# Second layer's down products written token-major, with gelu's output as the weights

## The chip, the cores and the metric

The kernel runs on one core of a Trainium2 chip. The metric is the device time of one execution in microseconds (us). A core has TensorE (in the profile PE for its products and PEld for its weight loads), VectorE (DVE), ScalarE (ACT), GpSimd (POOL) and SyncE (SP), which starts most transfers. The engines run their own instruction streams and meet only at semaphores.

## The reference

Four layers work on x, 4 samples of 256 tokens with 64 features. The change lies in the second half of the third one, a mixture of experts in which each sample picks two of eight experts for all its tokens:

```python
rw_tok = jnp.broadcast_to(routing_weights[:, None, :], (B, S, E)).reshape(N, E)
top_w, top_i = jax.lax.top_k(rw_tok, K)                  # K = 2
top_w = jax.nn.softmax(top_w, axis=-1)
h = jax.nn.gelu(jnp.einsum('nd,edf->enf', xf, W1) + b1[:, None, :], approximate=False)
y = jnp.einsum('enf,efd->end', h, W2) + b2[:, None, :]   # F = 128, D = 64
w_dense = jnp.zeros((N, E), x.dtype).at[jnp.arange(N)[:, None], top_i].add(top_w)
out = jnp.einsum('ne,end->nd', w_dense, y).reshape(B, S, D)
out = _layer_norm(out + x, gamma, beta)
```

Then `t = t + out`, and the fourth layer (attention with gates, then a second mixture of experts with one expert for each token) follows.

## The kernel before

Everything stays in the core's memory. A tensor is held either token-major (128 tokens down the partitions, 64 features along a row; a sample has TB = 2 such tiles) or feature-major (64 features down the partitions, 256 tokens along a row). Each engine's program is written out by hand, and every meeting of two engines is a counted semaphore. TensorE's program also holds products that nobody reads, with `onesb` as both operands (`keep_warm`), at fixed places and in fixed numbers.

The stage of the change, sample by sample (b = 0 to 3):

- Selection: ScalarE and VectorE copy the two chosen experts' matrices into `W1sel` (64 features and a bias row, by 128) and `W2sel` (128 by 64, already scaled with the expert's share `tw`). VectorE then works out `b2sel`, the mixed output bias, one column of 64 features for each sample.
- Up (L748): for each of the two experts one product, `W1sel` as the weights, the sample's tokens `XFb` (256 of them) moving. Result 128 by 256, twice, in one bank.
- Gelu (L1121, ScalarE): bank to `H2`, which lies in `bias_mem`.
- Down (L761): `W2sel` as the weights, `H2` moving, both experts added in the bank: 64 features by 256 tokens.
- Bias step (L1491, VectorE): bank plus `b2sel` to `UT`, which lies in `half_mem`.
- Turn (L770): two transposes through TensorE bring `UT` token-major into another bank.
- Sum (L1497, VectorE): turned bank plus `XNb` gives `U`, in `mid_mem`. After U of samples 0 to 2 VectorE takes the statistics of samples 0 and 1 (L1344, L1352, L1355), then U of sample 3, then the statistics of samples 2 and 3. GpSimd turns variances into factors (L405), and the two halves are normalised on VectorE (L1372) and ScalarE (L1051), scaled (L1509), added (L1511) and normalised again for the next layer.

An fp32 product is two instructions on TensorE, each with its own weight load; an fp32 transpose is one. GpSimd's addition at L437 (`X3b`) waits for the first bias step. Behind its last turn TensorE runs 34 `keep_warm` products (L453) and then `features_c` (L780), the turns for the next layer, as soon as their input is normalised. Names of the profile: `stack_mem` in this stage is `W1sel` and `W2sel`, `Cs` is the table of constants with the unit matrix `ident`.

Of the kernel before, what the change touches and what calls it, by code (L numbers as in the profile page):

```python
# [14 lines left out]
P = 128  # L15
B, HW, C = 4, 16, 64
N = HW * HW
TB = N // P
# [18 lines left out]
E2, F2, TOPK = 8, 128, 2  # L37
# [3 lines left out]
SLOTS = E3 * CAP3  # L41
# [5 lines left out]
IOTA_AT = NH * TB * SPAN // 2  # L47
# [4 lines left out]
ALU = mybir.AluOpType  # L52
# [24 lines left out]
def hybrid_kernel(nc, x, xt, w8, w0, wa, wg, w3, w2a, w2b, cst, bias_q, bias_k, lnw, out):  # L77
    ctx = ExitStack()
    with ctx:
# [5 lines left out]
        def sem(name):  # L85
            if name not in sems:
                sems[name] = ctx.enter_context(nc.semaphore(name))
            return sems[name]

        bank = [ctx.enter_context(nc.psum_tensor(f"bank{i}", [P, 512], F32)) for i in range(8)]  # L90
# [15 lines left out]
        half_mem = sb("half_mem", [P, 4992])  # L106
# [32 lines left out]
        ident = Cs[:, CST["ident"]]  # L139
# [79 lines left out]
        W2sel = view(stack_mem, P, B * TOPK, C)  # L219
        chosen = sb("chosen", [P, B * TOPK])  # L220
        b2w = sb("b2w", [C, B * TOPK, E2])
        b2sel = sb("b2sel", [C, B])
        H2 = view(bias_mem, P, B, TOPK * N)
        X4 = view(half_mem, P, T, C)
        UT = half_mem[0:C, IOTA_AT + SLOTS:IOTA_AT + SLOTS + B * N]
        U = view(mid_mem, P, T, C)
        gb = sb("gb", [P, 2, C])
        X3b = view(mid_mem, P, T, C)
# [125 lines left out]
        def _(pool):  # L354
# [77 lines left out]
                rstd("b", half)  # L432


            pool.wait_ge(sem("ut"), 1)
            pool.wait_ge(sem("gb_landed"), 16)
            pool.tensor_tensor(X3b[:, :, :], X3[:, :, :], gb[:, 1, :].unsqueeze(1).to_broadcast([P, T, C]), ALU.add) \  # L437
                .then_inc(sem("x3b"), 1)
# [9 lines left out]
        def _(pe):  # L448
# [138 lines left out]
            for t in range(T):  # L587
                last = pe.matmul(bank[7][:, t * C:t * C + C], XN1[:, t * P:t * P + P], W0s[:, W0["wv1"]],
                                 start=True, stop=True)
# [78 lines left out]
            for n in range(B * NH + LAG):  # L668
                b, h = divmod(n, NH)
# [31 lines left out]
            for i in range(B + 2):  # L701
# [9 lines left out]
                if 0 <= i - 1 < B:  # L711
                    b = i - 1
# [10 lines left out]
            for b in range(B):  # L723
# [14 lines left out]
                      start=True, stop=True).then_inc(sem("pe_routing"), 1)  # L738
            keep_warm(WARM["selection"], bank[7])

            for i in range(B + 2):
                if i < B:
                    b = i
                    pe.wait_ge(sem("sel_a"), 2 * b + 1)
                    pe.wait_ge(sem("sel_v"), 2 * b + 1)
                    pe.wait_ge(sem("b_xf"), B)
                    for k in range(TOPK):
                        last = pe.matmul(bank[b][:, k * N:k * N + N], W1sel[:, TOPK * b + k, :],  # L748
                                         XF["b"][:, b * N:b * N + N], start=True, stop=True)
                    last.then_inc(sem("up2"), 1)  # L750
                if 0 <= i - 1 < B:
                    b = i - 1
                    pe.wait_ge(sem("gelu"), b + 1)
                    pe.wait_ge(sem("sel_a"), 2 * b + 2)
                    pe.wait_ge(sem("sel_v"), 2 * b + 2)
                    if b == 0:
                        pe.wait_ge(sem("r_spread_read"), 2)
                    if b >= 2:
                        pe.wait_ge(sem("ut"), b - 1)
                    for k in range(TOPK):  # L760
                        last = pe.matmul(bank[4 + b % 2][0:C, 0:N], W2sel[:, TOPK * b + k, :],  # L761
                                         H2[:, b, k * N:k * N + N], start=(k == 0), stop=(k == TOPK - 1))
                    last.then_inc(sem("down2"), 1)
                if 0 <= i - 2 < B:
                    b = i - 2
                    pe.wait_ge(sem("ut"), b + 1)
                    if b >= 2:
                        pe.wait_ge(sem("u"), b - 1)
                    for q in range(TB):
                        last = pe.transpose(bank[6 + b % 2][:, q * C:q * C + C], UT[:, b * N + q * P:b * N + q * P + P],  # L770
                                            ident[0:C, 0:C])
                    last.then_inc(sem("u_turned"), 1)


            def features_c(b):
# [68 lines left out]
            for i in range(B + 2):  # L844
# [8 lines left out]
                if i >= 2:  # L853
                    pe.wait_ge(sem("d_xf"), i - 1)
                    for t in range(TB * (i - 2), TB * (i - 1)):
                        last = pe.matmul(bank[4][:, t * E3:t * E3 + E3], XF["d"][:, t * P:t * P + P],  # L856
                                         WAs[:, WA["gate"]], start=True, stop=True)
# [92 lines left out]
            for h in range(2):  # L950
                for q in range(T // 2):
                    t = h * T // 2 + q
                    if q % 2 == 0:
                        pe.wait_ge(sem("zt_v" if h else "zt"), q // 2 + 1)
                    last = pe.matmul(bank[h][:, q * C:q * C + C], ZT[:, t * P:t * P + P], twice[:, :],
                                     start=True, stop=True)
# [250 lines left out]
        def _(dve):  # L1207
# [264 lines left out]
            for i in range(1, B * TOPK, TOPK):  # L1472
# [10 lines left out]
                                   ALU.mult))  # L1483
            dve.tensor_reduce(b2sel[:, :], b2w[:, :, :].rearrange("p (b k) e -> p b (k e)", b=B), AX.X, ALU.add) \
                .then_inc(sem("b2sel"), 1)
            for i in range(B + 1):
                if i < B:
                    b = i
                    dve.wait_ge(sem("down2"), b + 1)
                    dve.wait_ge(sem("b2sel"), 1)  # L1490
                    dve.tensor_scalar(UT[:, b * N:b * N + N], bank[4 + b % 2][0:C, 0:N], b2sel[:, b:b + 1],  # L1491
                                      None, ALU.add) \
                        .then_inc(sem("ut"), 1)
                if i >= 1:
                    b = i - 1
                    dve.wait_ge(sem("u_turned"), b + 1)
                    dve.tensor_tensor(U[:, TB * b:TB * b + TB, :],  # L1497
                                      bank[6 + b % 2][:, 0:TB * C].rearrange("p (q c) -> p q c", q=TB),
                                      XN["b"][:, TB * b:TB * b + TB, 0:C], ALU.add).then_inc(sem("u"), 1)
                if i == B - 1:  # L1500
                    stats("u", U, "u", B // 2, 0)
# [268 lines left out]
```

## Time and profile before

| | us |
|---|---|
| median of 3 executions | 170.19 |
| lowest and highest | 169.01, 171.38 |
| the profiled execution | 168.97 |
| its span, first to last instruction | 167.1 |

| engine | busy, us | share of the span |
|---|---|---|
| PE | 146.9 | 88% |
| PEld | 102.9 | 62% |
| DVE | 111.3 | 67% |
| ACT | 75.1 | 45% |
| POOL | 50.8 | 30% |

A share of busy time is a mean over many short stages, and `keep_warm` counts as busy. All times below are from the start of the span; the stage of the change lies at 91 to 103 us.

### The profile page before, as it was taken

What the parts mean: (1) busy time and instruction counts of PE and PEld (TensorE: products, weight loads), DVE (VectorE), ACT (ScalarE), POOL (GpSimd) and SP (SyncE); (2) the same over time, 40 slices, a digit from 0 to 9 for tenths busy, and PEclk for the clock granted to TensorE, in tenths of its full rate; (3) what the DMA queues carried; (4) which work ended last, traced back from release to release, by engine and by line L of the source; (5) the groups of instructions that cost most, each with busy time, mean ns of one, the idle gap of its engine ahead of it and who ended that gap; (6) DMA issues with size and microseconds to landing.
All of it is one profiled execution on the core that took longest, in us unless ns stands there. A gap on an engine that the chain in (4) does not pass through costs nothing. (4 is left out here: it accounts for less than half of the span.)

```text
span 167.1 us, 3148 instructions
## 1 busy us (share of the span) xinstructions
PE 146.9 (88%) x1087; PEld 102.9 (62%) x1087; DVE 111.3 (67%) x385; ACT 75.1 (45%) x197; POOL 50.8 (30%) x78
## 2 busy tenths in 40 slices
PE   7999977799999998799787999967999899899920
PEld 2598736598888886588234554445665637678620
DVE  2027664987879898536644538947969289696873
ACT  3445605335353545451636550397535433555140
POOL 7051359786555657110400023520002200000000
PEclk9999999999999999999999999999999959999985
DMA  5993044373450000058000000000000000000002
GB/s 147 358 417 99 4 127 93 96 201 110 129 132 2 6 0 4 0 117 329 15 0 0 0 0 0 2 0 0 6 0 0 4 0 0 0 0 4 0 0 65
DMA packets 7098, 10.30 MB, mean 62 GB/s; under 512 B 2719, under 2 KB 5608, under 8 KB 6698
## 3 DMA queue, kind: packets, MB, share of 16 engines
q1 hardware_dynamic: 6880, 9.72, 19.2%
q10 hardware_dynamic: 202, 0.38, 0.9%
q8 instruction: 9, 0.15, 0.4%
q14 instruction: 7, 0.06, 0.1%
HBM read 8.52 MB, written 1.57 MB: 60 GB/s over the span
## 5 line engine op out<-in xcount | busy, mean ns | idle before, releaser
L453 PE MATMUL bank<-onesb 128*128 128x512 bf16 x142 | 36.7, 406 | 1.1 <-DVE onesb L1221 1.1
L453 PEld LDWEIGHTS bank<-onesb 128*128 128x128 bf16 x142 | 14.0, 105 | 16.1 <-issue 3.5
L418 POOL TENSOR_TENSOR half_mem<-identb,nm 128x256 bf16<-128x256 bf16 x32 | 19.5, 614 | 11.5 <-DVE nm L1302 11.3
L1302 DVE TENSOR_REDUCE nm<-bank 128x2 bf16<-128x352 f32 x32 | 16.3, 516 | 4.0 <-PE bank L607 3.7
L1037 ACT ACTIVATE mid_mem<-mid_mem 128x352 f32<-128x352 f32 x20 | 9.8, 496 | 18.4 <-DVE mid_mem L1313 18.4
L625 PE MATMUL bank<-stack_mem 72*128 72x176 bf16 x64 | 13.7, 240 | 0.1
L631 PE MATMUL bank<-half_mem,onesb 128*128 128x176 bf16 x64 | 13.5, 239 | 0.0
L605 PE MATMUL bank<-stack_mem 72*128 72x176 bf16 x64 | 12.7, 241 | 0.9 <-DVE nm L1302 0.9
L607 PE MATMUL bank<-half_mem,identb 128*128 128x176 bf16 x64 | 12.6, 239 | 0.0
L1313 DVE TENSOR_TENSOR mid_mem<-bank,bias_mem 128x352 f32<-128x352 f32 x20 | 10.3, 542 | 0.0
L629 PE MATMUL bank<-bias_mem,identb 128*128 128x176 bf16 x72 | 9.3, 238 | 0.0
L605 PEld LDWEIGHTS bank<-stack_mem 72*128 72x128 bf16 x64 | 6.2, 98 | 3.2 <-DVE nm L1302 2.1
L405 POOL TENSOR_TENSOR ln_rsd<-ln_ved,mhalf 128x4 f32<-128x4 f32 x2 | 2.1, 1027 | 18.1 <-DVE ln_ved L1355 18.1
L648 PE MATMUL bank<-mid_mem 128*32 128x176 f32 x128 | 6.4, 319 | 0.6 <-ACT mid_mem L1033 0.6
L625 PEld LDWEIGHTS bank<-stack_mem 72*128 72x128 bf16 x64 | 6.2, 97 | 0.6 <-issue 0.4
L1600 DVE TENSOR_SCALAR one_hot<-half_mem,sid 128x1280 fp32r<-128x1280 f32 x8 | 6.5, 882 | 0.0
L607 PEld LDWEIGHTS bank<-half_mem,identb 128*128 128x128 bf16 x64 | 6.3, 98 | 0.1
L1033 ACT ACTIVATE mid_mem<-bank 128x352 f32<-128x352 f32 x12 | 5.4, 454 | 1.7 <-PE bank L631 1.7
L631 PEld LDWEIGHTS bank<-half_mem,onesb 128*128 128x128 bf16 x64 | 6.2, 97 | 0.0
L1228 DVE TENSOR_REDUCE nmax<-bank 128x2 f32<-128x512 f32 x4 | 2.8, 688 | 5.1 <-PE bank L469 5.1
L923 PE MATMUL bank<-stack_mem,mid_mem 128*128 128x160 f32 x32 | 5.4, 312 | 0.8 <-ACT stack_mem L1162 0.7
L629 PEld LDWEIGHTS bank<-bias_mem,identb 128*128 128x128 bf16 x72 | 6.1, 98 | 0.0
(279 smaller groups left out, 330.8 us busy)
## 6 DMA issues: line engine op xcount, KB each, us to landing
stack_mem<-qk_parts SPq DMA_DIRECT2D x21, 96.0 KB
bias_mem<-bias_q SPq DMA_DIRECT2D x1, 1408.0 KB, 8.2
bias_mem<-bias_k SPq DMA_DIRECT2D x1, 1408.0 KB, 11.7
mid_mem<-w SPq DMA_DIRECT2D x1, 1024.0 KB, 7.5
qk_parts<-half_mem SPq DMA_DIRECT2D x4, 192.0 KB, 2.7
qk_parts<-half_mem SPq DMA_DIRECT2D x4, 128.0 KB, 2.4
mid_mem<-w2b SPq DMA_DIRECT2D x1, 512.0 KB, 8.4
Cs<-cst SPq DMA_DIRECT2D x1, 336.0 KB, 4.3
```

Source lines behind the costliest of these rows:

```text
L418: pool.tensor_tensor(diag1[:, b % 2, h, :].rearrange("p (q k) -> p q k", q=TB), identb[:, :].unsqueeze(1).to_broadcast([P, TB, P]), nm1[:, ...
L453: pe.matmul(idle[:, :].rearrange("p (k q) -> p k q", k=4), onesb[:, :], onesb[:, :].unsqueeze(1).to_broadcast([P, 4, P]), start=True, stop ...
L605: pe.matmul(dst, QS[:, b, h, q * P:q * P + P], KSt[:, b, h, OFF[q]:OFF[q] + SPAN], start=True, stop=False)
L607: last = pe.matmul(dst, identb[:, :], biasQb[:, h, q * SPAN:q * SPAN + SPAN], start=False, stop=True)
L625: pe.matmul(dst, KSt[:, b, h, k * P:k * P + P], QS[:, b, h, OFF[k]:OFF[k] + SPAN], start=True, stop=False)
L629: pe.matmul(dst, identb[:, :], bias_part[:, i, PE_HEADS.index(h), span], start=False, stop=False)
L631: last = pe.matmul(dst, onesb[:, :], diag1[:, b % 2, h, OFF[k]:OFF[k] + SPAN], start=False, stop=True)
L648: last = pe.matmul(bank[4 + b % 2][32 * g:32 * g + VW, c0 + OFF[k]:c0 + OFF[k] + SPAN], V1[:, TB * b + k, h, :], P1[:, (b * NH + h) % (2 * ...
L1037: act.activation(P1[:, n % (2 * QUAD), :], U1[:, n % 3, :], ACT.Exp).then_inc(sem("p1"), 1)
L1302: dve.tensor_reduce(nm1[:, n // NH, n % NH, :], bank[n % 2][:, 0:TB * SPAN].rearrange("p (q k) -> p q k", q=TB), AX.X, ALU.max, negate=Tru ...
L1313: dve.tensor_tensor(U1[:, n % 3, :], bank[2 + n % 2][:, 0:TB * SPAN], biasK[:, n % NH, :], ALU.add) \
L1600: dve.tensor_scalar(G3[:, t % 3, :], iota_f[:, :], sid[:, t:t + 1], None, ALU.is_equal) \
```

## The change

The operands of the down product change places: a block of 128 tokens of `H2` is the weights, and `W2sel` with its 64 columns moves. The result is token-major at once, so the turn and VectorE's step into `UT` go. The bias enters as one more product into the same bank: `b2sel`'s column, repeated 128 times by a stride of zero, as the weights, and the 64 by 64 unit matrix moving, once for both token blocks (128 columns) and ahead of the down products; for sample 0 it comes behind them, once for each block of tokens, with a wait for `b2sel` behind the first block. The sum at L1497 now waits for the down product itself, and GpSimd's L437 for the first U in place of the first bias step.

```diff
-            pool.wait_ge(sem("ut"), 1)
+            pool.wait_ge(sem("u"), 1)
...
-            for i in range(B + 2):
+            for i in range(B + 1):
...
                     if b >= 2:
-                        pe.wait_ge(sem("ut"), b - 1)
-                    for k in range(TOPK):
-                        last = pe.matmul(bank[4 + b % 2][0:C, 0:N], W2sel[:, TOPK * b + k, :],
-                                         H2[:, b, k * N:k * N + N], start=(k == 0), stop=(k == TOPK - 1))
+                        pe.wait_ge(sem("u"), b - 1)
+                    dst = bank[6 + b % 2][:, 0:TB * C].rearrange("p (q c) -> p q c", q=TB)
+                    bias, unit = b2sel[:, b:b + 1].to_broadcast([C, P]), ident[0:C, 0:C]
+                    if b > 0:
+                        pe.matmul(dst, bias, unit.unsqueeze(1).to_broadcast([C, TB, C]), start=True, stop=False,
+                                  skip_group_check=True)
+                    for q in range(TB):
+                        for k in range(TOPK):
+                            last = pe.matmul(dst[:, q, :], H2[:, b, k * N + q * P:k * N + q * P + P],
+                                             W2sel[:, TOPK * b + k, :], start=(b == 0 and k == 0),
+                                             stop=(b > 0 and k == TOPK - 1), skip_group_check=True)
+                        if b == 0:
+                            if q == 0:
+                                pe.wait_ge(sem("b2sel"), 1)
+                            last = pe.matmul(dst[:, q, :], bias, unit, start=False, stop=True, skip_group_check=True)
                     last.then_inc(sem("down2"), 1)
-                if 0 <= i - 2 < B:
-                    b = i - 2
-                    pe.wait_ge(sem("ut"), b + 1)
-                    if b >= 2:
-                        pe.wait_ge(sem("u"), b - 1)
-                    for q in range(TB):
-                        last = pe.transpose(bank[6 + b % 2][:, q * C:q * C + C], UT[:, b * N + q * P:b * N + q * P + P],
-                                            ident[0:C, 0:C])
-                    last.then_inc(sem("u_turned"), 1)
...
-            for i in range(B + 1):
-                if i < B:
-                    b = i
-                    dve.wait_ge(sem("down2"), b + 1)
-                    dve.wait_ge(sem("b2sel"), 1)
-                    dve.tensor_scalar(UT[:, b * N:b * N + N], bank[4 + b % 2][0:C, 0:N], b2sel[:, b:b + 1],
-                                      None, ALU.add) \
-                        .then_inc(sem("ut"), 1)
+            for i in range(1, B + 1):
                 if i >= 1:
                     b = i - 1
-                    dve.wait_ge(sem("u_turned"), b + 1)
+                    dve.wait_ge(sem("down2"), b + 1)
```

TensorE's program from the last two up products to the 34 products that nobody reads, before (a row is one product in the program; `[waits ...]` are the semaphores ahead of it):

```order
412 L748 MATMUL bank<-XFb,stack_mem 128x256 [waits b_xf,sel_v,sel_a]
413 L748 MATMUL bank<-XFb,stack_mem 128x256
414 L761 MATMUL bank<-bias_mem,stack_mem 64x256 [waits sel_v,ut,sel_a,gelu]
415 L761 MATMUL bank<-bias_mem,stack_mem 64x256
416 L770 MATMUL bank<-Cs,half_mem 128x64 [waits ut]
417 L770 MATMUL bank<-Cs,half_mem 128x64
418 L761 MATMUL bank<-bias_mem,stack_mem 64x256 [waits sel_v,ut,sel_a,gelu]
419 L761 MATMUL bank<-bias_mem,stack_mem 64x256
420 L770 MATMUL bank<-Cs,half_mem 128x64 [waits u,ut]
421 L770 MATMUL bank<-Cs,half_mem 128x64
422 L770 MATMUL bank<-Cs,half_mem 128x64 [waits u,ut]
423 L770 MATMUL bank<-Cs,half_mem 128x64
```

And TensorE's program now, from sample 0's down product to the same place (L747 is the up product, L766 the down product, L762 and L772 the bias):

```order
404 L766 MATMUL bank<-stack_mem,bias_mem 128x64 [waits sel_v,r_spread_read,sel_a,gelu]
405 L766 MATMUL bank<-stack_mem,bias_mem 128x64
406 L772 MATMUL bank<-Cs,b2sel 128x64 [waits b2sel]
407 L766 MATMUL bank<-stack_mem,bias_mem 128x64 x2
408 L772 MATMUL bank<-Cs,b2sel 128x64
409 L747 MATMUL bank<-XFb,stack_mem 128x256 [waits b_xf,sel_v,sel_a]
...
414 L747 MATMUL bank<-XFb,stack_mem 128x256
415 L762 MATMUL bank<-Cs,b2sel 128x128 [waits sel_v,u,sel_a,gelu]
416 L766 MATMUL bank<-stack_mem,bias_mem 128x64 x4
417 L762 MATMUL bank<-Cs,b2sel 128x128 [waits sel_v,u,sel_a,gelu]
418 L766 MATMUL bank<-stack_mem,bias_mem 128x64 x4
```

The turns are gone, the down product has become five products in place of two, and sample 0's holds a wait for `b2sel` in its middle.

VectorE's program from `b2sel` to the end of the first statistics, before:

```order
178 L1484 TENSOR_REDUCE b2sel<-b2w 64x4
179 L1491 TENSOR_SCALAR half_mem<-bank,b2sel 64x256 x2
180 L1497 TENSOR_TENSOR mid_mem<-bank,XNb 128x128
181 L1491 TENSOR_SCALAR half_mem<-bank,b2sel 64x256
182 L1497 TENSOR_TENSOR mid_mem<-bank,XNb 128x128
183 L1491 TENSOR_SCALAR half_mem<-bank,b2sel 64x256
184 L1497 TENSOR_TENSOR mid_mem<-bank,XNb 128x128
185 L1344 BN_STATS ln_stu<-mid_mem 128x6 x4
```

And now (L1491 is here the sum U, and L1345 the statistics):

```order
178 L1485 TENSOR_REDUCE b2sel<-b2w 64x4
179 L1491 TENSOR_TENSOR mid_mem<-bank,XNb 128x128 x3
180 L1345 BN_STATS ln_stu<-mid_mem 128x6 x4
181 L1353 BN_AGGR ln_mvu<-ln_stu 128x2 x4
182 L1356 TENSOR_SCALAR ln_veu<-ln_mvu 128x4
183 L1491 TENSOR_TENSOR mid_mem<-bank,XNb 128x128
```

The four bias steps are gone; the sums and the statistics keep their order, and sample 3's bias step no longer stands ahead of sample 2's sum.

## Rows read from the trace of the kernel before

**Rows 1.** The page's head and TensorE's granted clock in 40 slices (tenths).

```profile
span 167.1 us, 3148 instructions
...
PEclk9999999999999999999999999999999959999985
```

**Rows 2.** The chain that ended last, in order of time: start us, length us, what.

```profile
93.99 1.08 PE bank L761 x4
95.07 1.06 PE bank L748 x4
96.13 1.01 PE bank L761 x4
97.14 0.27 PE bank L770 x2
...
99.74 1.02 PE bank L761 x4
...
100.78 0.48 DVE half_mem L1491
101.26 0.20 DVE mid_mem L1497
...
138.68 3.20 PE bank L877 x15
```

**Rows 3.** Timeline, 93 to 103 us: start us, us, engine, line, out<-in, [idle before].

```profile
94.49 0.21 DVE L1484 TENSOR_REDUCE b2sel<-b2w 64x4 f32<-64x64 f32 x1
...
95.66 1.26 POOL L437 TENSOR_TENSOR mid_mem<-X,gb 128x512 f32<-128x512 f32 x1 [13.57 <-DVE half_mem L1491]
...
98.50 0.60 ACT L1121 ACTIVATE bias_mem<-bank 128x512 f32<-128x512 f32 x1 [1.74 <-PE bank L748]
...
101.18 0.27 DVE L1497 TENSOR_TENSOR mid_mem<-bank,XNb 128x128 f32<-128x128 f32 x1
...
101.58 6.65 PE L453 MATMUL bank<-onesb 128*128 128x512 bf16 x30
...
102.42 0.17 DVE L1355 TENSOR_SCALAR ln_veu<-ln_mvu 128x4 f32<-128x4 f32 x1
102.49 0.28 DVE L1497 TENSOR_TENSOR mid_mem<-bank,XNb 128x128 f32<-128x128 f32 x1
```

**Rows 4.** Timeline, 105 to 110 us.

```profile
105.53 0.42 DVE L1511 TENSOR_TENSOR half_mem<-stack_mem,mid_mem 128x256 f32<-128x256 f32 x1
...
105.69 3.40 PE L453 MATMUL bank<-onesb 128*128 128x512 bf16 x15
...
108.78 1.65 ACT L1051 ACTIVATE stack_mem<-half_mem,ln_nbc,ln_rsc 128x128 f32<-128x128 f32 x4 [1.76 <-POOL ln_nbc L409]
...
109.80 0.41 PE L780 MATMUL bank<-Cs,stack_mem 128*128 128x128 f32 x2 [0.71 <-ACT stack_mem L1051]
```

**Rows 5.** Timeline at 74 and at 159 us: products with 128 weight columns and few moving ones.

```profile
74.27 1.08 PEld L697 LDWEIGHTS bank<-XNa,S_PT 128*128 128x128 f32 x8
74.48 1.00 PE L697 MATMUL bank<-XNa,S_PT 128*128 128x65 f32 x8
...
75.52 0.17 DVE L1414 RECIPROCAL rdena<-bank 128x2 f32<-128x2 f32 x1 [2.00 <-PE bank L697]
...
159.09 0.97 PEld L955 LDWEIGHTS bank<-twice,XHL 128*128 128x128 f32 x8 [0.97 <-issue]
```

**Rows 6.** Groups by line and form: count, busy us, mean ns, idle before.

```profile
L697 PEld LDWEIGHTS bank<-XNa,S_PT 128*128 128x128 f32 x32 | 4.1, 192 | 0.2
...
L761 PEld LDWEIGHTS bank<-bias_mem,stack_mem 128*64 128x64 f32 x16 | 1.9, 136 | 2.2 <-ACT bias_mem L1121 0.8 <-issue 0.7
```

**Rows 7.** Windows: us, busy us and instructions of each engine, clock, DMA share, GB/s.

```profile
94.00:98.00 4.00, 4.00 (x17) 2.41 (x18) 1.78 (x6) 1.01 (x2) 1.26 (x1) 1.00 0.00 0
...
134.00:136.00 2.00, 2.00 (x15) 0.79 (x13) 1.83 (x9) 0.26 (x1) 0.00 (x0) 0.55 0.00 0
136.00:138.00 2.00, 2.00 (x7) 0.78 (x6) 1.90 (x7) 1.11 (x4) 0.00 (x0) 0.60 0.00 0
```

**Rows 8.** Timeline, 136 to 144 us: VectorE's comparisons for the gather at L877.

```profile
136.88 6.49 DVE L1600 TENSOR_SCALAR one_hot<-half_mem,sid 128x1280 fp32r<-128x1280 f32 x8
```

More of the change, by code:

```diff
@@ L224, in hybrid_kernel @@
         X4 = view(half_mem, P, T, C)
-        UT = half_mem[0:C, IOTA_AT + SLOTS:IOTA_AT + SLOTS + B * N]
         U = view(mid_mem, P, T, C)
```

## The prediction

> **What bounds the kernel now.** Four views, in this order. The page's head gives the span, 167.1 us, and shows that TensorE's clock was at its upper level nearly everywhere [rows 1]. The chain of work that ended last says who holds the stage of the change: from 93.99 us it runs through TensorE alone, without a gap, over down, up, down, turn, up, down, turn, down (1.08, then 1.06 for each of two up products, 1.01 for each further down product, 0.27 for each of two turns), until 100.76 us; then over VectorE's bias step of sample 3 (0.48) into the sum U of sample 2, which began at 101.18 us [rows 2, 3]. From there VectorE holds the chain with the statistics. The timeline shows what stands close beside it, and the windows give the clock. So this stage is bound by TensorE up to U of sample 2, and then by VectorE. Each tenth of a microsecond by which U of sample 2 starts earlier is one for the whole kernel, if nothing named below is late in its place.
>
> The profiled execution took 168.97 us, 1.87 more than its span and 1.22 less than the median of 170.19. I work out a difference on the profiled execution and take it off the median.
>
> **The change part by part.**
>
> *Removed from the path.* Two turns, 2 x 0.27 = 0.54 us; VectorE's bias step of sample 3 ahead of sample 2's sum, 0.48 us less what overlaps (the sum began 0.40 us after that step did) [rows 2, 3]. The other three bias steps ran beside TensorE's products and give nothing.
>
> *Changed on the path.* A down product was four instructions (two products, two for fp32 each) with 256 moving columns in 1.01 us. It becomes eight with 64 moving columns, and two for the bias with 128 columns. The trace has the same form elsewhere. L697 has 128 weight columns and 65 moving ones: eight weight loads took 1.08 us, of which the last is 0.192 long [rows 5, 6]; so from one to the next (1.08 - 0.192) / 7 = 0.127 us. L955 has 64 moving columns: (0.97 - 0.192) / 7 = 0.111 us [rows 5, 6]. I take 0.12, between the two, and call it p. The bias product's instructions have the same number of weight columns and 128 moving; a column of an fp32 instruction costs 1.01 / (4 x 256), about 1 ns [rows 2], so the stream would want 0.13 and I count them as p too. A stride of zero in the weights has no row in this trace; its bounds are p and, if such loads could not run ahead at all, the 0.192 of a whole load. Four instructions on the path up to U of sample 2 (of samples 1 and 2) could so cost up to 4 x 0.07 = 0.3 us more, and four of sample 0 as much again. I take p, since all other loads with 128 columns in fp32 run under the products before them.
>
> The size of a load is where a page has something to say against this change. Loads of 64 columns lasted 136 ns here and loads of 128 columns 192 ns [rows 6]. The Trainium skill, in "TensorE: Matmul & The Clock Gate", section "LDWEIGHTS (loading the stationary operand)", says that a load's time goes with the number of weight columns and not with the contraction, about columns / 1.2 ns; by that rule exchanging the operands makes each load dearer by 53 ns, and the trace agrees with 56. The same rule, taken as the spacing of a stream bound by loads, would be 0.107 us.
>
> *Added to the path.* In sample 0's down product TensorE waits for `b2sel` behind its first four instructions. These start at 93.99 us, with gelu, and are through their loads at 94.35 + 0.12. `b2sel` starts at 94.49 and takes 0.21 [rows 3]: 94.70, and 0.04 for the signal. So eight instructions stand behind 94.74 us. Behind this wait in TensorE's queue are the second token block and the up products of samples 2 and 3, and ScalarE's gelu of samples 2 and 3 waits for those.
>
> *The sum.* By this the next up product starts at 94.74 + 8p, and U of sample 2 at 94.74 + 8p (rest of sample 0) + 1.06 (up) + 10p (sample 1) + 1.06 (up) + 9p (up to the last load of sample 2) + 0.36. The last term is the time from the last load to VectorE's start at L697: the last load began at 74.27 + 7 x 0.127 = 75.16, VectorE at 75.52 [rows 5]. Together 97.22 + 27p. With p = 0.12 that is 100.46 us where it was 101.18: a gain of 0.7 us. With 0.127 it is 0.5, with 0.111 it is 1.0.
>
> *What is late next.* Three covers are thin.
> - U of sample 3 can start at 97.22 + 37p = 101.66 us. VectorE reaches it behind the first statistics, formerly at 102.49 [rows 3], now 0.7 earlier, at 101.8: covered by 0.1.
> - The 34 products that nobody reads start behind sample 3's down product, at 96.86 + 38p = 101.4 us, formerly at 101.58. They last as before, to 105.69 + 3.40 = 109.09 less 0.2, so 108.9. The next layer's turn, formerly at 109.80 behind ScalarE [rows 4], is due at 109.1: covered by 0.2. TensorE stood idle 0.71 us there, so no gain much above 0.9 could come through this place.
> - Gelu of sample 3 ran at 98.50, beside TensorE [rows 3]; it moves behind the later up product, to about 99.1 to 99.7. Sample 3's down product is due at 100.3. Covered by 0.6; uncovered it would cost one for one.
>
> *Free of charge.* GpSimd's addition at L437 waits for U of sample 0 in place of the first bias step: from 95.66 to about 96.3, over at 97.6; L1511, which reads it, runs at 105.53 [rows 3, 4], and GpSimd's next work, the first factors, comes at 102 us. Its cover is some 4 us. No transfer and no queue of SyncE is touched.
>
> **The rivals.**
>
> *Exposed loads, the one that ends slower.* Every new down instruction carries its own load of 128 columns and streams 64, so the load is longer than the stream (0.192 against about 0.065). If a load did not run under the product before it, p would be 0.192: U of sample 2 at 97.22 + 27 x 0.192 = 102.4, U of sample 3 at 104.3 against 102.49, and the products that nobody reads would start 2.6 late against 0.71 of idle time. The largest delay, 1.9 us, would come through: 172.1 us. It decides from p = 0.142 to 0.147, where these terms equal the times of before. Against it: 0.111 and 0.127 in rows 5. For it: weights that are gelu's fresh output, repeated columns in every step, and the exchange of two weight regions (64 rows for the bias, 128 for the rest). Chance 0.07.
>
> *A shorter spacing.* The Trainium skill, in the section "Back-to-back issue gap" of the page named above, gives about 81 ns for a load and product pair in a stream with 128 columns, against 0.111 and 0.127 us in rows 5, which are fp32. What such a spacing would do here: with p = 0.08, U of sample 2 comes at 99.4, a gain of 1.8, of which sample 3's later product and the next turn let most pass, since those 34 products would begin 1.7 earlier as well. That is 168.4 us. The rows speak against it, with L697 and L955 both above 0.11. Chance 0.05.
>
> *The clock falls elsewhere.* In the profiled execution the clock was low once, over parts of 134 to 136 and 136 to 138 us, a granted 0.55 and 0.60 [rows 7], so at 1.2 GHz for some 3.4 us in all; ahead of it TensorE had short turns and products with 8 columns. There it cost next to nothing, since TensorE waited for VectorE anyway. VectorE's comparisons then pace the gather at 6.49 / 8 = 0.81 us each [rows 8], while TensorE needs 2.5 x 3.20 / 15 = 0.53 at full clock [rows 2], and 1.07 at half. Were the low stretch to fall on the gather, its 3.4 us would lose 3.4 / 0.81 x (1.07 - 0.81) = 1.1 us. The executions of before spread over 2.4 us, and the profiled one was the fastest; a shift by 0.7 us can put more or fewer of them there. With the gain in it: 169.5 + 1.1 = 170.6 us. Chance 0.17. In 94 to 98 us the clock was full [rows 7]; as the products of 65 columns at 74 us kept it, I expect no fall within the stage.
>
> *Nothing comes through.* The wait for `b2sel`, the slower bias loads and the two thin covers each take a few tenths and leave 0.0 to 0.2: 170.1 us. Chance 0.13.
>
> **How the numbers follow.** The forecast, a gain of 0.7 on 170.19, is 169.5 us, chance 0.58; its own range is 168.7 to 170.2, from a gain of 0.5 to 1.0 and half a microsecond for a median of three runs that lie 2.4 apart. The range that should hold 8 times in 10 adds the clock and the lost gain: 168.3 to 171.2. Two per cent, 3.4 us, is about what a measurement of this kernel can tell from no change; neither of the named cases reaches 166.8 or 173.6. For what I have not seen I leave 0.03 on the fast side and 0.03 on the slow one, and 0.94 within.
>
> **What the profile of the changed kernel would show.** The loads of the down product at 0.11 to 0.13 us from one to the next, and the bias instructions no slower. Sample 0's down product interrupted at about 94.5 and on from 94.74, the next up product 0.6 us later than before. U of sample 2 at about 100.5, U of sample 3 straight behind the first statistics, with VectorE idle before it for under 0.1. The first factors on GpSimd 0.7 earlier. At the next layer's turn an idle time of about 0.2 where there was 0.71, ended by ScalarE. From there the same rows as before, shifted by 0.7. The prediction is wrong if loads of the broadcast column are slow, if TensorE is still busy with the products that nobody reads when ScalarE has the next layer's input, or if the clock's low stretches fall on other work in most executions of one kernel and not of the other.

## The result, and the profile after

The changed kernel took 176.83 us in the median of 4 executions (175.07 to 181.83), the kernel before 170.22 (169.01 to 171.38). The ratio is 1.0355, 95% interval 1.0234 to 1.0475: slower by 3.5%, where 169.5 us and a small gain were forecast. Ratios here leave out executions more than 1.5% above the fastest of their kernel, and with them some of those in which the clock fell, so where the spread itself is the finding, I give all times.

The head of the page after, to be held against [rows 1]:

```profile
span 175.3 us, 3174 instructions
...
PEclk9999999999999999999999555699999999999995
```

The clock was low in the middle, where it had been full. The chain that ended last, through the stage (start us, length us, what), against [rows 2]:

```profile
95.34 0.48 PE bank L772 x2
95.83 1.04 PE bank L766 x4
96.87 0.62 PE bank L772 x2
97.49 2.00 PE bank L747 x4
99.49 0.72 PE bank L762 x2
100.22 1.90 PE bank L766 x8
102.11 1.81 PE bank L747 x4
103.93 0.72 PE bank L762 x2
104.65 1.90 PE bank L766 x8
106.55 0.72 PE bank L762 x2
107.27 1.90 PE bank L766 x8
109.17 9.12 PE bank L452 x34
118.29 0.23 PE bank L781 x2
```

TensorE holds the chain as before, but an up product (L747), which the change does not touch, takes 2.00 and 1.81 us where it took 1.06. The windows name the reason (busy us and instructions of PE, PEld, DVE, ACT, POOL; then the granted clock, DMA share, GB/s), against [rows 7]:

```profile
92.00:95.50 3.50, 2.99 (x16) 2.20 (x14) 1.93 (x10) 2.60 (x8) 0.00 (x0) 1.00 0.00 0
95.60:99.00 3.40, 3.40 (x12) 2.64 (x11) 0.29 (x1) 0.00 (x0) 1.10 (x1) 0.50 0.00 0
99.00:102.40 3.40, 3.40 (x13) 2.71 (x12) 0.25 (x1) 0.60 (x1) 0.16 (x1) 0.50 0.00 0
102.40:105.80 3.40, 3.40 (x12) 2.40 (x10) 0.04 (x1) 1.82 (x2) 0.00 (x0) 0.50 0.00 0
105.80:109.20 3.40, 3.40 (x15) 2.97 (x15) 1.35 (x10) 0.26 (x2) 1.02 (x1) 0.50 0.02 5
109.20:112.60 3.40, 3.40 (x9) 1.21 (x8) 3.23 (x17) 0.30 (x1) 1.36 (x2) 0.50 0.00 0
112.70:116.00 3.30, 3.30 (x17) 1.50 (x16) 3.09 (x21) 1.54 (x6) 1.38 (x2) 1.00 0.00 0
```

From 95.6 us, one microsecond into the stage, TensorE ran at 1.2 GHz, through the whole stage and into the products that nobody reads, and was back at 2.4 GHz only there. From the fall on it counts as busy without a gap. Where the 8.2 us of span went: the stage began at 94.58 us in place of 93.99 (0.6, from work ahead of it that the change leaves alone); from its first down product to the products that nobody reads 14.4 us in place of 7.6 (6.8); from there to the next layer's turn, now at 118.13, 9.2 in place of 8.2 (0.9); from there to the end 57.2 in place of 57.3.

The timeline shows the stage's start, where the clock fell, against [rows 3]:

```profile
94.58 0.52 PEld L766 LDWEIGHTS bank<-stack_mem,bias_mem 128*128 128x128 f32 x4 [0.80 <-ACT bias_mem L1122]
...
95.34 0.30 PEld L772 LDWEIGHTS bank<-Cs,b2sel 64*128 64x128 f32 x2 [0.24 <-DVE b2sel L1485]
```

Ahead of the fall TensorE idled for gelu, ran four thin instructions (loads of 0.52 us in all, so (0.52 - 0.19) / 3 = 0.11 us apart, as forecast) and stopped again for `b2sel`. So only one microsecond of changed instructions lay ahead of the fall; the up products and the wait for gelu ahead of them stand in the kernel before too, where the clock stayed up.

### The profile page after: what moved, and what is told of

Read it like the earlier page. It is cut to its first block and busy times, and to the rows that moved or that the text cites. A ratio compares the mean times of both kernels' runs of the same rounds, so it can differ in the third digit from the quotient of the medians.

```text
span 175.3 us, 3174 instructions
## 1 busy us (share of the span) xinstructions
PE 155.5 (89%) x1105; PEld 110.7 (63%) x1105; DVE 109.7 (63%) x381; ACT 75.1 (43%) x197; POOL 50.8 (29%) x78
## 5 line engine op out<-in xcount | busy, mean ns | idle before, releaser
L452 PE MATMUL bank<-onesb 128*128 128x512 bf16 x142 | 37.6, 414 | 1.0 <-DVE onesb L1222 1.0
L452 PEld LDWEIGHTS bank<-onesb 128*128 128x128 bf16 x142 | 14.4, 107 | 16.6 <-issue 4.3
L1491 DVE TENSOR_TENSOR mid_mem<-bank,XNb 128x128 f32<-128x128 f32 x4 | 1.2, 292 | 11.9 <-PE bank L766 9.7
L766 PE MATMUL bank<-stack_mem,bias_mem 128*128 128x64 f32 x32 | 7.7, 411 | 0.4 <-ACT bias_mem L1122 0.4
L766 PEld LDWEIGHTS bank<-stack_mem,bias_mem 128*128 128x128 f32 x32 | 6.8, 309 | 1.6 <-ACT bias_mem L1122 0.8
L878 PE MATMUL bank<-one_hot,XHL 128*128 128x512 f32 (+1 forms) x24 | 6.1, 382 | 0.3 <-DVE one_hot L1594 0.3
```

The source lines that it names most:

```text
L452: pe.matmul(idle[:, :].rearrange("p (k q) -> p k q", k=4), onesb[:, :], onesb[:, :].unsqueeze(1).to_broadcast([P, 4, P]), start=True, stop ...
L766: last = pe.matmul(dst[:, q, :], H2[:, b, k * N + q * P:k * N + q * P + P], W2sel[:, TOPK * b + k, :], start=(b == 0 and k == 0), stop=(b ...
L878: last = pe.matmul(bank[c][:, 0:width], XHL[:, t, :, :].rearrange("p k c -> p (k c)"), G3[:, t % 3, at:at + width], start=(t == 0), stop=( ...
```

## The experiments

Four suspects: the thin streams of the down product (A), the stop for `b2sel` (B), the repeated bias column as weights (C), and, after the first four runs, the change of rows at the bias product (D). Below, "the stage" is the time from the first down product to the first of the 34 products that nobody reads, in the profiled execution: 7.6 us before, 14.4 after. "Low" is a granted clock of 0.5, 1.2 GHz.

**The changed kernel again.** No edit.

> The changed kernel as it is, once more, beside the others. All theories: 175 to 178 us in most executions, mean granted clock 0.93 to 0.95, as in its first four.

Measured: 174.91, 174.99, 176.22, 176.41 and 181.29 us; ratio to the kernel before 1.0299 (1.0238 to 1.0359). With the first four, nine executions and none below 174.9. In the profiled one, of 181.29 us, the clock had been low once before, long ahead of the change (10.6 to 31.1 us), which made the stage 7 us late. It fell again at 106.2 us, inside the stage (first down product at 101.77), and the stage took 11.6 us:

```profile
PEclk9965555999999999999999985599999999999995
```

**Streams of double width.** The second copy falls into columns that nobody reads.

```diff
-dst = bank[6 + b % 2][:, 0:TB * C].rearrange("p (q c) -> p q c", q=TB)
+both = bank[6 + b % 2][:, 0:TB * 2 * C].rearrange("p (q w c) -> p q w c", q=TB, w=2)
+dst = both[:, :, 0, :]
...
-last = pe.matmul(dst[:, q, :], H2[...], W2sel[:, TOPK * b + k, :], ...)
+last = pe.matmul(both[:, q, :, :], H2[...], W2sel[:, TOPK * b + k, :].unsqueeze(1).to_broadcast([P, 2, C]), ...)
```

> The changed kernel with each down product streaming 128 columns in place of 64: the expert's 64 columns twice, the second copy into a part of the bank that nobody reads. Loads, waits and order are unchanged, the result too. Thin streams (theory A: the clock falls because the stage's products stream few columns behind long loads): the clock stays at its upper level through the stage, the stage takes what was forecast (U of sample 2 about 6.5 us behind the first down product), 169 to 171 us. The wait (theory B: TensorE's stop for b2sel in sample 0's down product makes it fall) or the repeated bias column (theory C): the low stretch stays, 175 to 178 us.

Measured: 169.71, 171.43, 171.48 and 174.96 us; ratio 1.0051 (0.9957 to 1.0146). Doubling the columns that TensorE streams, with nothing else changed, takes away most of the loss in three executions of four. In the profiled one, of 174.96, the clock still fell in the stage, at 98.0 us (first down product at 95.16). So A has a part, but is not all of it.

**Sample 0's bias behind its down products.** No stop in the middle.

```diff
-                        if b == 0:
-                            if q == 0:
-                                pe.wait_ge(sem("b2sel"), 1)
-                            last = pe.matmul(dst[:, q, :], bias, unit, start=False, stop=True, ...)
+                    if b == 0:
+                        pe.wait_ge(sem("b2sel"), 1)
+                        last = pe.matmul(dst, bias, unit.unsqueeze(1).to_broadcast([C, TB, C]), start=False, stop=True, ...)
```

> The changed kernel with sample 0's bias as one product behind its four down products, so that b2sel is there before TensorE comes to it; two bias instructions fewer and next to no stop in the middle. Theory A (thin streams): still slow, some tenths of a microsecond less than the changed kernel, 174.5 to 177.5. Theory B (the wait): full clock in the stage and 169 to 170.5 us. Theory C (the repeated column): as A.

Measured: 174.29, 174.47, 176.05 and 181.97 us; ratio 1.029 (1.0196 to 1.0385). As A and C had it: without the stop the clock still fell in the stage, in the profiled execution at 106.1 us, 3.1 us behind the first down product. It was low from 10.6 to 31.0 us as well, as in the repeat of the changed kernel.

**The stop alone, in the kernel before.**

```diff
                     for k in range(TOPK):
+                        if b == 0 and k == 1:
+                            pe.wait_ge(sem("b2sel"), 1)
                         last = pe.matmul(bank[4 + b % 2][0:C, 0:N], W2sel[...], H2[...], ...)
```

> The kernel before with one wait more: TensorE waits for b2sel between the two products of sample 0's down product. All else is as before. Theory A (thin streams) and C (repeated column): the clock as in the kernel before, the wait costs at most some 0.2 to 0.4 us, 169.5 to 171.5. Theory B (the wait alone lets the clock fall): a low stretch in the stage, 173 to 177 us.

Measured: 169.15 to 171.40 us, ratio 1.0003 (0.992 to 1.0085). The stop costs the stage 0.3 us (7.9 for 7.6) and, among streams of 256 columns, does not bring the clock down. B alone is out.

**No bias products.** The kernel leaves out the output bias, and with it the stop for `b2sel`.

```diff
-                    if b > 0:
-                        pe.matmul(dst, bias, unit..., start=True, stop=False, ...)
...
-                        if b == 0:
-                            if q == 0:
-                                pe.wait_ge(sem("b2sel"), 1)
-                            last = pe.matmul(dst[:, q, :], bias, unit, start=False, stop=True, ...)
```

> The changed kernel without the bias products and without the wait for b2sel; the output bias of the second layer's experts is left out of the computation. Theory C (the repeated column as weights): full clock, 168 to 170 us. Theory B (the wait): the same. Theory A (thin streams of 64 columns): the clock still falls in the stage, 173 to 176.5 us, lower than the changed kernel by the ten bias instructions, 1 to 2 us at low clock.

Measured: 168.09, 168.64, 168.85 us and one of 179.53 at a mean clock of 0.991, so disturbed by something else than the clock; ratio 0.9913 (0.9838 to 0.9988). A alone is out, as far as three executions tell: the streams are as thin as in the changed kernel, and in the profiled one the clock stayed up in the stage, which took 5.4 us:

```profile
PEclk9999999699999999999999999999999969999975
```

As taking the stop away did not help by itself, the bias product matters, and its row says how. In the run with both early edits (next but one), at full clock:

```profile
97.81 0.29 PEld L763 LDWEIGHTS bank<-Cs,b2sel 64*128 64x128 f32 x2 [0.33 <-issue]
97.81 0.48 PE L763 MATMUL bank<-Cs,b2sel 64*128 64x128 f32 x2
...
98.22 0.19 PEld L767 LDWEIGHTS bank<-stack_mem,bias_mem 128*128 128x128 f32 x1
98.22 0.38 PE L767 MATMUL bank<-stack_mem,bias_mem 128*128 128x128 f32 x1
```

The first load of the bias and the first load behind it start together with their products, where the loads between them start ahead, beside the product before. Two instructions take 97.81 to 98.22 = 0.41 us, where I had 0.24. The bias is over 64 rows, the products around it over 128 and 65. That was theory D: the change of rows keeps the loads from running ahead.

**The bias over 128 rows.**

```diff
-        b2sel = sb("b2sel", [C, B])
+        b2sel = sb("b2sel", [P, B])
...
-                    bias, unit = b2sel[:, b:b + 1].to_broadcast([C, P]), ident[0:C, 0:C]
+                    bias, unit = b2sel[:, b:b + 1].to_broadcast([P, P]), ident[:, 0:C]
...
+            dve.memset(b2sel[C:P, :], 0.0).then_inc(sem("b2sel_low"), 1)
```

> The changed kernel with the bias product over all 128 rows: b2sel gets 64 rows of zeros below, and the first 64 columns of the full unit matrix move. As many instructions, columns and loads, the same wait in sample 0, the same result. Theory D (a product with 64 rows between products with 128 rows cannot have its weights loaded ahead, nor can the one behind it, which costs some 0.3 us a sample and lets TensorE stream so little that the clock falls): the two bias instructions take 0.11 us each, the clock stays up in the stage in most executions, 169 to 171 us. Theory C (the repeated column itself): loads as slow as before and the clock low, 175 to 178 us. Theory A (thin streams alone): the gaps go but the clock still falls, 174 to 176 us.

Measured: twelve executions in two groups, five at 169.52 to 170.61 us and seven at 173.75 to 177.14, with mean clocks of 0.959 to 0.977 and 0.920 to 0.947; the median is 174.24. So D's edit alone frees less than half of the executions. In the profiled one, of 174.99, the clock fell at 95.8 us, 1.1 us behind the first down product.

**Double width and sample 0's bias behind.** The bias at 64 rows.

> The changed kernel with both edits of the first two runs: each down product streams its 64 columns twice, and sample 0's bias is one product behind its down products. The bias stays at 64 rows. If the fall of the clock goes by how much of the stage TensorE streams, two edits that each raise that share keep the clock up more often than either alone: 169.5 to 171 us with the slow switches of rows still in it. If the bias product as such lets the clock fall: 172 us or more.

Measured: eight executions at 168.38 to 169.86 us, one at 176.30 and one at 181.47 (the latter at a mean clock of 0.985); ratio 0.9912 (0.9859 to 0.9966). The bias product as such does not bring the clock down. In the profiled execution the stage took 7.8 us at full clock, no less than in the kernel before.

**The bias over 128 rows, sample 0's behind.** Streams of 64 columns.

> The changed kernel with the bias product over 128 rows and sample 0's bias as one product at the end, so neither switch of rows nor stop in the middle; the streams of the down product stay at 64 columns. Theory D (switches of rows): full clock and what was forecast, 168.5 to 170 us, U of sample 2 some 6.1 us behind the first down product. Theory A (thin streams alone): the clock falls, 173 to 175 us.

Measured: eight executions at 167.60 to 170.66 us, two at 175.54 and 176.81; ratio 0.9935 (0.9876 to 0.9993). The profiled execution, 167.60 us, is the changed kernel's idea at full clock. The clock of its page, and its timeline:

```profile
PEclk9999999999999999999999999999999999999995
...
93.96 0.97 PEld L766 LDWEIGHTS bank<-stack_mem,bias_mem 128*128 128x128 f32 x8 [0.80 <-ACT bias_mem L1123]
...
96.05 0.39 PE L762 MATMUL bank<-Cs,b2sel 128*128 128x128 f32 x2
96.16 0.97 PEld L766 LDWEIGHTS bank<-stack_mem,bias_mem 128*128 128x128 f32 x8
...
96.27 1.00 PE L766 MATMUL bank<-stack_mem,bias_mem 128*128 128x64 f32 x8
...
99.29 0.29 DVE L1493 TENSOR_TENSOR mid_mem<-bank,XNb 128x128 f32<-128x128 f32 x1 [1.69 <-PE bank L766]
...
100.21 7.50 PE L452 MATMUL bank<-onesb 128*128 128x512 bf16 x34
...
100.63 0.28 DVE L1493 TENSOR_TENSOR mid_mem<-bank,XNb 128x128 f32<-128x128 f32 x1
...
107.93 0.41 PE L782 MATMUL bank<-Cs,stack_mem 128*128 128x128 f32 x2 [0.22 <-ACT stack_mem L1053]
```

Two bias instructions take 0.22 us (96.05 to 96.27), and the load behind them starts 0.11 ahead of its product. The stage takes 6.2 us, U of sample 2 starts 5.3 us behind the first down product in place of 7.2, and the next layer's turn 13.96 in place of 15.81, a gain of 1.85 us. Of these 1.4 reach the span (165.7 us for 167.1): from that turn to the end it took 57.8 us in place of 57.3. A load of the repeated column lasts as long as any other, by the groups of the same kernel:

```profile
L766 PEld LDWEIGHTS bank<-stack_mem,bias_mem 128*128 128x128 f32 x32 | 3.9, 192 | 0.8 <-ACT bias_mem L1123 0.8
L762 PEld LDWEIGHTS bank<-Cs,b2sel 128*128 128x128 f32 x6 | 1.1, 191 | 0.1
```

That is the end of C.

**The kernel before with a product of 64 rows more.** Its result is read by nobody.

```diff
+                    pe.matmul(bank[4 + b % 2][:, 256:384].rearrange("p (q c) -> p q c", q=TB), ident[0:C, :],
+                              ident[0:C, 0:C].unsqueeze(1).to_broadcast([C, TB, C]), start=True, stop=True)
                     for k in range(TOPK):
```

> The kernel before with one product more ahead of each sample's down product: 64 rows, unit matrices as both operands, 128 columns, into a part of the bank that nobody reads. Theory D: each costs 0.5 to 0.55 us in place of the 0.26 that two instructions of 128 columns would take if their loads ran ahead, about 1.6 us on the path up to U of sample 2; if the share of streaming then suffices, the clock stays up and the time is 171 to 172.5 us; if not, it falls and the time is 174 to 178. Theory A or C: full clock and a cost of 0.8 us on the path, 170.5 to 171.5.

Measured: nine executions at 170.19 to 173.09 us and one at 183.34 (mean clock 0.990); ratio 1.0086 (1.003 to 1.0143). In the profiled execution the clock stayed up in the stage, and the stage took 8.7 us in place of 7.6 (9.1 from the first extra product on):

```profile
99.02 0.48 PE L760 MATMUL bank<-Cs 64*128 64x128 f32 x2
99.44 1.08 PE L763 MATMUL bank<-bias_mem,stack_mem 128*64 128x256 f32 x4
...
103.36 0.44 PE L760 MATMUL bank<-Cs 64*128 64x128 f32 x2
```

An extra product takes 0.42 us (99.02 to 99.44), less than the 0.5 to 0.55 expected, and neither its load nor the one behind runs ahead. The last one, at 103.36, stands behind a turn, which has 64 rows too, and its load does run ahead: it starts at 103.30. So the price of the rows holds in the old form too; but there the down product streams 256 columns for each load, and the clock stayed up. D alone is not enough either.

**All three edits.**

> The changed kernel with all three edits: bias over 128 rows, sample 0's bias behind its down products, and each down product streaming its 64 columns twice. If the clock's fall goes by how little TensorE streams in the stage (theory D), this one streams most and the clock falls in the stage in no execution or nearly none; as the second copy costs some 0.01 to 0.02 us an instruction, the stage takes 6.3 to 6.5 us, and the time is 168 to 169.5 us. If something else than streaming decides, it falls as often as with 64 columns (3 of 10 executions).

Measured: six executions, 167.21 to 170.45 us, median 168.96; ratio 0.9897 (0.9848 to 0.9946). Stage 6.3 us, with the clock up. This is no measurable step beyond the three kernels with 0.9912 to 0.9935 and overlapping intervals (the run without bias, 0.9913, among them), although its stage is 1.5 us shorter than that with 64 rows.

**All three, and one product that nobody reads where TensorE waits for gelu.**

```diff
+                    if b == 0:
+                        keep_warm(1, bank[4])
                     pe.wait_ge(sem("gelu"), b + 1)
```

> As the run with all three edits, and one product of 512 columns that nobody reads where TensorE waits for sample 0's gelu, some 0.4 us of idle time, so that it costs nothing. If idle time ahead of the stage helps the clock to fall, this one falls less often; the time is otherwise the same within 0.3 us, 168 to 169.5 us.

Measured: twelve executions, 167.00 to 170.37 us, median 169.29; ratio 0.9908 (0.9864 to 0.9951). With the six above, eighteen executions and none above 170.5. The extra product shows no effect; as the kernel without it showed no fall either, this run can't tell whether idle time has a part.

**Work added to the changed kernel.**

```diff
                     last.then_inc(sem("down2"), 1)
+                    if b < B - 1:
+                        keep_warm(3, bank[4])
```

> The changed kernel with work added: three products of 512 columns that nobody reads behind each of the first three down products. At full clock they cost 9 x 0.216 = 1.9 us, so the stage would be some 1 us longer than in the kernel before. Theory D (share of streaming): the clock stays up in most executions and the kernel becomes faster than the changed one by this added work, 171 to 173.5 us. If the clock falls for another reason (the repeated column, the 64-row product, the wait): slower still, 178 us or more.

Measured: 172.22, 173.43, 173.89, then 179.78, 179.84 and 187.90 us. Half of the executions became faster than any of the changed kernel by adding 1.9 us of work, the other half slower. In the profiled one, of 179.78, the clock was low from 97.8 to 114.9 us, from the end of the first three added products on. It cuts both ways as a remedy, as each of the two outcomes that were expected came in some of the executions, but the first three can't be had by any theory in which only the changed instructions' own length counts.

## Why the prediction was wrong

The step that failed is the last sentence of the rival on the clock: "as the products of 65 columns at 74 us kept it, I expect no fall within the stage". I had the clock as something that might move about elsewhere, worth 1.1 us, and took one row at 74 us as proof for the stage. The clock fell inside the stage in both profiled executions of the changed kernel, and nine of nine had the time that goes with it. In the first of them the way from the first down product to the next layer's turn took 23.55 us in place of 15.81. Without the fall it would have been about 16.0, an estimate: 15.35 in the run with double width and sample 0's bias behind, and 0.6 for the stop and sample 0's second bias (from the first down product to the next up product 95.16 to 97.28 us with the stop, 95.25 to 96.75 without). So some 7.6 us are the clock's.

The same estimate shows a second step that failed, smaller and independent of the clock: 16.0 against 15.81 is a loss of 0.2 where 0.7 of gain was forecast. That is the bias product, below.

What brought the clock down is no single part. The table counts executions by time: every one above 173.7 us with a mean clock under 0.96 is counted as low, and those of 179.5 us and more with a mean clock of 0.98 and more are left out. Where no profile was taken, that the fall lay in the stage is inferred, not shown.

| kernel | streams | bias rows | stop in sample 0 | low, of |
|---|---|---|---|---|
| changed | 64 | 64 | yes | 9 of 9 |
| changed, with products added | 64 and 512 | 64 | yes | 4 of 6 |
| bias behind | 64 | 64 | no | 4 of 4 |
| bias over 128 rows | 64 | 128 | yes | 7 of 12 |
| double width | 128 | 64 | yes | 1 of 4 |
| 128 rows, bias behind | 64 | 128 | no | 2 of 10 |
| double width, bias behind | 128 | 64 | no | 1 of 9 |
| no bias products | 64 | none | no | 0 of 3 |
| all three edits (two kernels) | 128 | 128 | no | 0 of 18 |
| before, with the stop | 256 | none | yes | 0 of 4 |
| before, with 64 rows more | 256 | 64 | no | 0 of 9 |

The kernel before has such executions too: by the same rule 3 of 30, 1 of 7, none of 17 and none of 4 in its four series, 4 of 58. So the last seven rows can't be told from it, nor from each other. What the counts show is this. Double width keeps the clock up in most executions at 64 bias rows, with the stop (1 of 4 against 9 of 9; chance alone would give that 1 time in 70) and without it (1 of 9 against 4 of 4). So does the bias over 128 rows once the stop is gone (2 of 10 against 4 of 4); beside the stop it does so in part (7 of 12 against 9 of 9, 1 time in 26). That the stop has a part is not shown: at 64 rows taking it away changed nothing, and at 128 rows 7 of 12 against 2 of 10 can be chance, 1 time in 12. The run with products added counts 4 of 6 only with its execution of 173.89 us, at a clock of 0.951, which lay near the border.

These edits have in common that TensorE streams more of the stage's time, one by more columns, one by loads that run ahead again. That this is what keeps the clock up fits the counts, but is argued: no run changes it alone, and the added products of 512 columns, which raise it too, left the clock low in half of the executions or more. Why two executions of one kernel differ stays open.

*The spacing of the down product* was right: 0.11 us between loads, in the changed kernel and at full clock in the run with 128 rows, against my 0.111 to 0.127 and the 0.12 taken. The 0.127 was a misreading: the first of the eight loads at L697 began early, under a product of 256 columns (load at 74.27, product at 74.48 us), and from the second on they stand 0.111 apart in that trace.

*The bias product* was mis-sized. "I count them as p too": 0.24 us a sample. At 64 rows it takes 0.41 us, and begins 0.09 late on top (0.31 us behind the up product's last instruction in place of 0.216, from the starts in that trace); together 0.50. At 128 rows it is 0.22. The reason given, "since all other loads with 128 columns in fp32 run under the products before them", was wrong in the trace of before, where the loads of the turn and of the up product behind it start with their products:

```profile
96.76 0.38 PE L761 MATMUL bank<-bias_mem,stack_mem 128*64 128x256 f32 x1
97.07 0.20 PEld L770 LDWEIGHTS bank<-Cs,half_mem 64*128 64x128 f32 x2 [0.38 <-issue]
97.07 0.33 PE L770 MATMUL bank<-Cs,half_mem 64*128 64x64 f32 x2
...
97.33 0.30 PEld L748 LDWEIGHTS bank<-XFb,stack_mem 65*128 65x128 f32 x2
97.33 0.48 PE L748 MATMUL bank<-XFb,stack_mem 65*128 65x256 f32 x1
```

I had named "the exchange of two weight regions (64 rows for the bias, 128 for the rest)" among the reasons for exposed loads, at a chance of 0.07 and for all ten instructions; it holds for the loads at the two borders. With it the forecast gain would have been gone: 3 x 0.26 = 0.8 us against 0.7, and sample 0 has the borders twice.

At full clock with 64 rows and sample 0's bias behind, the next layer's turn came 15.35 us behind the first down product, against 15.81 before, a gain of 0.46; at 128 rows the gain is 1.85, more than twice the forecast, with three terms of my sum too long. Without the stop and with two bias instructions fewer, the first up product starts 1.21 us behind the first down product in place of 1.71. An up product takes 0.87 us (95.18 to 96.05 us in that run's timeline) where I carried 1.06 over from before, twice. And the spacing is 0.111 for 0.12, some 0.2 over 19 loads.

*The stop for `b2sel`* was as worked out: the bias began at 95.34 us, 0.76 behind the first down product, with `b2sel` done at 95.30, against a forecast 0.75.

*The thin covers* held at full clock: U of sample 3 stood straight behind the first statistics, and TensorE's idle time ahead of the next turn was 0.22 us, against some 0.2 forecast, though for a larger gain.

*The rival of exposed loads* gave the sign and, at 172.1 us, not the size; its rows in the changed kernel (loads 0.21 us apart behind 95.6) look like it, but are the half clock: the same loads stand 0.11 apart ahead of that time.

The Trainium skill, in "TensorE: Matmul & The Clock Gate", section "Step-by-step: what each phase is for", has a load run ahead of products in flight when the row groups don't conflict, or when it goes to the background weight buffer. The traces agree for 65 beside 128 rows and for 128 beside 128, as long as both have 128 weight columns. For 64 beside 128 rows and back they show no load ahead, though the second case would seem to allow it; nor do they in the kernel before between the up product (65 rows, 128 weight columns) and the old down product (128 rows, 64 weight columns), 0.31 us for 0.216. Here the measurement decides.

## What to carry to other kernels

Ask of a changed stage what clock it will be granted, and don't take busy time for an answer: here TensorE was busy from end to end at half the clock. An exchange of operands that puts the short side on the moving end can keep the length of the stage and still cost its clock, and the price falls on neighbours that nobody touched. One row elsewhere that kept the clock is no proof for another stage.

A small product with fewer rows than its neighbours costs two exposed loads; rows of zeros, up to the neighbours' count, took them away here. Before counting a load as hidden, look at a border of the same kind in the trace: does the load start ahead of its product, or with it?

The idea of the change pays, about 1%, with both mended: bias over 128 rows and behind sample 0's products, each stream doubled, 0.990 of the kernel before (0.985 to 0.995). That the doubled streams are needed beside the other two edits is not shown (2 of 10 low without them, none of 18 with them).

## What the runs showed of the hardware

- Two fp32 instructions with 128 weight columns and 128 moving ones take 0.22 us among products of as many rows, and 0.41 us with 64 rows among products with 128 and 65. A product of 64 rows behind another of 64 rows has its load 0.06 us ahead.
- No load ran ahead either between fp32 products with 128 and with 64 weight columns (65 and 128 rows): 0.31 us from the last instruction to the next product, in place of 0.216. Whether the columns or the rows are the reason was not tested.
- A stride of zero in the weights costs nothing: 191 ns a load against 192.
- Streaming 128 columns in place of 64 behind an fp32 load of 128 columns is nearly free: the stage took 6.3 us in place of 6.2, although twice as much went through TensorE.
- Once low, the clock stayed low for 17 us in the changed kernel's profile (95.6 to 112.6), over up products that stream 256 columns each, until 3.7 us into the products that nobody reads; for 10 us in its repeat (106.2 to 116.4).
- It fell without a long idle time: in the changed kernel's profile TensorE's longest idle stretches between 86 us and the fall were 0.87 us, up to 89.58, and 0.40 us, up to 94.58, and the kernel before has both (0.86 and 0.40) and kept the clock.
